# A DiT block with experts: the instruction lists ahead of the main loop in a new order

## The chip, the cores and the metric

One core of a Trainium2 chip. The metric is the device time of one execution in microseconds, the median of several runs. A kernel here is one program written engine by engine: TensorE (PE in the profile), VectorE (DVE), ScalarE (ACT), GpSimd (POOL) and SyncE (SP, which issues the loads and stores) each run a list of instructions in order, and semaphores hold an instruction until what it needs is there.

## The reference

Four sequences of 1024 tokens with 256 channels go through two layers, all in float32:

```python
m = silu(mod) @ w_ada + b_ada              # nine modulation rows per batch
h = ln(x) * (1 + sc_msa) + sh_msa
x = x + self_attn(h) * g_msa               # 16 heads, windows of 128, rolled by 64
h = ln(x) * (1 + sc_mca) + sh_mca
x = x + topk_cross_attn(h, context) * g_mca  # 77 keys, softmax over the 16 largest scores
h = ln(x) * (1 + sc_mlp) + sh_mlp
x = x + swiglu(h) * g_mlp                  # hidden 1024
# second layer
nx = layer_norm(x, gamma, beta)
evidence = softmax(nx @ Wq @ (ctx @ Wk).T / 16) @ (ctx @ Wv)
combined = concat(nx, evidence, cond)
p = softmax(combined @ router_W + router_b)          # three experts
routed = sum_e p_e * (silu(combined @ e_w1[e] + e_b1[e]) @ e_w2[e] + e_b2[e])
g = sigmoid(silu(combined @ gate_w1 + gate_b1) @ gate_w2 + gate_b2)
out = x + g * (routed @ out_w + out_b)
```

## The kernel before, in words

The 4096 tokens are 16 units of 256 tokens (two tiles of 128). A unit passes three stages: A (self-attention), C (cross-attention with the search for the 16 largest of 77 scores) and B (SwiGLU, then the experts). The main loop, `both`, runs stage A of one unit, C of the unit before and B of the one before that side by side. Ahead of the loop `prologue` takes unit 0 through A and C and unit 1 through A, and meanwhile prepares the weights. Only this part is changed.

What is prepared, the "folds": the nine modulations from the condition vector ("mS" for the first norm, "mR" for the others, lines 1014 and 1024); the gate rows of the three residuals ("g25", "g8") and the value biases through the output weights ("bv"); the second expert weights multiplied by the output weight, for which they are first turned ("t00" to "t21", line 688) and then multiplied ("p00" to "p21", line 696); the experts' output biases through the output weight ("b01", "b2", line 645); the turned wk and wq and their product ("wk", "wq", "MT"); the condition's part of the experts' first layer ("anchor", line 674) and of the router ("r0", then "r1", lines 628 and 637).

Three things set the order of the work:

- each engine's list is written out by hand: the calls in `prologue` of TensorE (line 1011), ScalarE (1504), GpSimd (1860) and VectorE (2321). A call that waits holds everything behind it on its engine;
- the eight PSUM banks. Banks 5 to 7 go round among the folds in the order of `FOLD_JOBS` (line 404): a fold may begin when the one three places ahead of it has been read out. `FOLDS_DONE` gives the order in which TensorE ends them. Banks 0 to 4 belong to the stages, in the order of `PRO_JOBS` (line 65): in bank 1 the values of unit u ("v") are followed by slot 1 of its scores ("s01"), so the scores (line 817) wait until ScalarE has copied the values out (line 1394);
- SP's list (line 444). Once VectorE has made the gate rows (line 2034, signal `rows_gated`), SP stores them in device memory and reloads them spread over the partitions, then loads the weights of stage B; once the expert rows are halved (line 2052, `expert_rows`) it stores and reloads these and loads the evidence weights and the down weights.

Self-attention of a unit goes like this: scores into banks 0 to 3 (four slots of four heads), row maxima by VectorE (line 2148), exponentials with row sums by ScalarE (line 1400, sixteen per tile), probabilities turned by TensorE (line 835) and copied out by ScalarE (line 1409), products with the values (line 858). The inverse row sums are spread over the channels by GpSimd (line 1773), turned by TensorE (line 861), copied by ScalarE and multiplied in by VectorE (line 2179); then the projection (line 872). GpSimd's list has, ahead of the first spread, the gating of two output weights with the reloaded gate rows (lines 1862 to 1868). In cross-attention the scores are copied out (line 1424), searched by VectorE in two halves per slot (line 2202: the eight largest, knock them out, the next eight), shifted by GpSimd, put through the exponential by ScalarE (line 1429) and masked by VectorE ("pick", line 2226). `idle_in_values` and `idle_products` (lines 1000 to 1009) are products of the identity whose results nobody reads.

At the end of the prologue, TensorE turns the last probabilities of unit 1 with the router rows between them, and the router rows wait until VectorE has read "r0" (line 640), which stands behind all of unit 0's searches in VectorE's list:

```python
                a_turn_probs(1, 2, 1)
                fold_router_rows()
                a_turn_probs(1, 3, 1)
                wait_folds(pe)
                idle_products(5)
                a_turn_inverses("r1", "pv", 1)
                a_values(1, 1)
```

Of the kernel before, what the change touches and what calls it, by code (L numbers as in the profile page):

```python
# [144 lines left out]
def bass_pixart_experts(nc, x, cond, ctx_in, w_ada, b_ada, w_qkv, b_qkv, w_so, b_so, w_q, b_q, w_kv, b_kv,  # L145
# [6 lines left out]
    with ExitStack() as stack:  # L152
# [182 lines left out]
        def wait_free(eng, name, u):  # L335

            eng.wait_ge(drained[JOB[name][0]], before(name, u) + 1)
# [51 lines left out]
        def every_batch(dst, v):  # L389
# [15 lines left out]
            "cols", "mS", "cT", "cK", "cV", "mR", "bv", "g25", "g8", "t01", "t00", "b01",  # L405
            "anchor", "p00", "p01", "t10", "t11", "b2", "wk", "p11", "p10", "wq", "t20", "t21",
# [3 lines left out]
            "cols", "mS", "cT", "cK", "cV", "mR", "bv", "g25", "g8", "t01", "t00", "b01",  # L410
            "p00", "p01", "anchor", "t10", "t11", "b2", "wk", "p11", "p10", "wq", "t20", "t21",
# [12 lines left out]
        def fold_psum(name):  # L424
            return psum[5 + FOLD_BANK[name]]
# [153 lines left out]
        def _(pe):  # L579
# [116 lines left out]
            def fold_second(e, k2):  # L696

                pe.wait_ge(out_scaled, 1)
                wait_read(pe, f"t{e}0")
                wait_read(pe, f"t{e}1")  # L700
                bk = fold_bank(f"p{e}{k2}")
                for k in (2 * k2, 2 * k2 + 1):
                    for h in range(CB):
                        m = pe.matmul(bk[:, (k % 2) * C:(k % 2 + 1) * C], e2T[h][:, k * P:(k + 1) * P], outw[:, h, :],
                                      start=(h == 0), stop=(h == CB - 1))
                m.then_inc(fold_full, 1)
# [304 lines left out]
            def prologue():  # L1011
# [9 lines left out]
                a_v(0, 0)  # L1021
                context_values(0, fold_bank("cV"))
                a_v(1, 0)
                modulations("mR", (4, 3, 7, 6))
                a_scores(0, range(SLOTS), 0)
                value_biases()
                gate_sections("g25", (0, 1))
                a_turn_probs(0, 0, 0)
                a_turn_probs(0, 1, 0)
                gate_sections("g8", (2,))  # L1030
                a_turn_probs(0, 2, 0)
                fold_turn_second(0, 1)
                a_turn_probs(0, 3, 0)
                fold_turn_second(0, 0)
                fold_expert_biases("b01", (0, 1))
# [4 lines left out]
                idle_in_values(3)  # L1040
                a_turn_probs(1, 1, 0)
                fold_second(0, 0)
                a_turn_probs(1, 2, 0)
                a_turn_probs(1, 3, 0)
                fold_second(0, 1)
# [13 lines left out]
                fold_turn("wk", wk_sb)  # L1059
                pe.wait_ge(readA, 2)  # L1060
                a_cross_scores(0, range(SLOTS), 0)
                wait_free(pe, "pv", 1)
                idle_in_values(2)
                a_turn_input(1)
                idle_in_values(5)
                a_cross_scores(1, range(SLOTS), 0)
# [3 lines left out]
                a_v(0, 1)  # L1070
                fold_second(1, 1)
                a_v(1, 1)
                fold_second(1, 0)
                a_scores(0, range(SLOTS), 1)
# [3 lines left out]
                fold_qk()  # L1078
                a_turn_probs(0, 0, 1)
                fold_router_anchor()  # L1080
                idle_in_values(2)
# [5 lines left out]
                idle_in_values(6)  # L1087
                a_scores(1, range(SLOTS), 1)
                a_values(0, 1)
                fold_second(2, 1)  # L1090
                fold_second(2, 0)
                a_turn_probs(1, 0, 1)
# [264 lines left out]
        def _(act):  # L1357
# [146 lines left out]
            def prologue():  # L1504
# [13 lines left out]
                a_copy_turned(0, 3, 0, "p")  # L1518
                read_fold("t00", e2T[0], fold_psum("t00")[:, :])
                read_fold("t01", e2T[1], fold_psum("t01")[:, :])  # L1520
# [28 lines left out]
                a_kept_exp(0, 0)  # L1549
# [9 lines left out]
                a_copy_turned(0, 3, 1, "p")  # L1559
                a_cross_exp(1, 0, 0)  # L1560
                read_fold("t21", e2T[1], fold_psum("t21")[:, :])
                a_cross_exp(1, 1, 0)
# [4 lines left out]
                a_exp(1, 3, 1)  # L1567
                a_copy_turned(1, 0, 1, "p")
# [1101 lines left out]
```

## Time and profile before

| | |
|---|---|
| device time, median of 3 runs | 1445.8 us (1445.67 to 1449.09) |
| the profiled execution | span 1447.1 us, 30246 instructions; the page gives no other time of it |
| first matmul of the loop (line 920) | 126.78 us after the span's start |
| PE busy | 1413.0 us, 98% |
| DVE busy | 1061.7 us, 73% |
| ACT busy | 837.8 us, 58% |
| POOL busy | 437.8 us, 30% |
| chain that ended last, by engine | PE 83%, DVE 12%, issue 2%, ACT 1% |

"Busy" is time in which an engine executes an instruction. In a timeline, a row is one instruction or several like ones in a row: its start, how long, the engine, the line, the operation with its output and inputs, how many; in brackets how long the engine stood idle before it and who released it. A matmul of float32 shows as two instructions. Starts of consecutive rows may lie closer than the durations, since matmuls overlap at their ends. In a table by stretch each engine has its busy time and its count of instructions, then come the granted share of TensorE's clock (PEclk, 1.00 is 2.4 GHz, 0.50 is 1.2 GHz), the share of the DMA engines and the GB/s.

### The profile page before, as it was taken

How to read it: one execution, taken by the hardware profiler on the slowest of the kernel's cores; microseconds unless marked ns; L12 is line 12 of the kernel's file. 1: busy time of each engine (PE TensorE's matmuls, PEld its weight loads, DVE VectorE, ACT ScalarE, POOL GpSimd, SP SyncE). 2: the span in 40 equal slices, each digit the busy share in tenths (PEclk: the TensorE clock that was granted, in tenths of full speed). 3: DMA queues.
4: the chain of work that ended last, by engine and by line, in shares of the span. 5: the costliest groups of instructions: out<-in, count | busy, mean ns of one | idle time of the engine just before them, and what ended most of it. 6: DMA issues, size and time to landing. Idle time of an engine off the chain costs nothing.

```text
span 1447.1 us, 30246 instructions
## 1 busy us (share of the span) xinstructions
PE 1413.0 (98%) x9777; PEld 1195.1 (83%) x9777; DVE 1061.7 (73%) x4754; ACT 837.8 (58%) x2555; POOL 437.8 (30%) x599
## 2 busy tenths in 40 slices
PE   7999999999999999999999999999999999999997
PEld 5778788888888888888888788888888878887886
DVE  3585869688796878879696777959688786968642
ACT  3464475757566384755757466574757547574433
POOL 1314132333325232332335232233334313232302
PEclk9999999999999999999999999999999999999999
DMA  7520000010000000010010000000010000000000
GB/s 244 196 73 2 1 1 25 1 34 9 19 31 15 1 2 25 2 34 2 21 36 2 15 2 16 11 15 20 8 43 8 16 2 1 9 2 8 1 2 14
DMA packets 27342, 34.99 MB, mean 24 GB/s; under 512 B 3325, under 2 KB 22449, under 8 KB 26930
## 3 DMA queue, kind: packets, MB, share of 16 engines
q1 hardware_dynamic: 27185, 33.07, 7.1%
q8 instruction: 79, 1.29, 0.4%
q14 instruction: 78, 0.63, 0.1%
HBM read 28.83 MB, written 4.22 MB: 23 GB/s over the span
## 4 chain that ended last, share of the span: by engine, by line
PE 83%; DVE 12%; issue 2%; ACT 1%; SPq 0%; POOL 0%; DMA 0%; DVEq 0%; ACTq 0%; POOLq 0%
PE bank L965 13%; PE bank L920 12%; PE bank L989 10%; PE bank L972 7%; PE bank L791 6%; PE bank L929 6%; PE bank L777 4%; PE bank L852 4%; PE bank L840 4%; PE bank L904 4%; DVE knocked L2224 3%; PE bank L830 2%; PE bank L748 2%; PE bank L762 2%; PE bank L812 1%
## 5 line engine op out<-in xcount | busy, mean ns | idle before, releaser
L920 PE MATMUL bank<-hB,Wm 128*128 128x256 f32 x1024 | 242.3, 383 | 2.2 <-ACT hB L1366 2.2
L920 PEld LDWEIGHTS bank<-hB,Wm 128*128 128x128 f32 x1024 | 190.6, 190 | 33.4 <-issue 7.0
L965 PE MATMUL bank<-nxT,W1nx 128*128 128x256 f32 x896 | 212.1, 382 | 0.0
L1405 ACT ACTIVATE prob<-bank,rmax 128x128 f32<-128x128 f32 x512 | 180.3, 432 | 28.3 <-DVE rmax L2151 28.3
L1762 POOL TENSOR_TENSOR scores<-scores,M 128x308 f32<-128x308 f32 x128 | 94.5, 738 | 320.1 <-DVE knocked L2224 317.7
L1412 ACT ACTIVATE probT<-bank 128x512 f32<-128x512 f32 (+1 forms) x256 | 140.3, 617 | 83.8 <-PE bank L904 76.8
L989 PE MATMUL bank<-W2p,gT 128*128 128x256 f32 x768 | 183.2, 381 | 3.0 <-DVE acc L2303 1.9
L965 PEld LDWEIGHTS bank<-nxT,W1nx 128*128 128x128 f32 x896 | 166.1, 191 | 23.1 <-issue 2.8
L989 PEld LDWEIGHTS bank<-W2p,gT 128*128 128x128 f32 x768 | 141.2, 190 | 23.8 <-issue 2.8
L1450 ACT ACTIVATE tbs<-bank,b1half 128x256 f32<-128x256 f32 x128 | 60.7, 474 | 143.1 <-PE bank L920 102.2
L1466 ACT ACTIVATE tbs<-bank,betaH 128x256 f32<-128x256 f32 x224 | 95.6, 489 | 82.7 <-PE bank L972 82.7
L1405 ACT ACTIVATION_READ_ACCUMULATOR prob<-bank,rmax 128x1 f32 x512 | 139.0, 272 | 0.0
L1754 POOL TENSOR_SCALAR vare<-mv 128x2 f32<-128x2 f32 x64 | 17.7, 276 | 385.1 <-DVE mv L2127 382.7
L929 PE MATMUL bank<-Wm_g,gT 128*128 128x256 f32 x480 | 115.2, 380 | 0.0
L972 PE MATMUL bank<-wT,Vp 77*128 77x256 f32 x448 | 114.0, 382 | 0.0
L2224 DVE MATCH_REPLACE8 knocked<-M,scores 128x77 f32<-128x77 f32 x512 | 108.7, 226 | 0.9 <-issue 0.5
L2224 DVE MATCH_REPLACE8 knocked<-M,knocked 128x77 f32<-128x77 f32 x512 | 108.8, 227 | 0.7 <-issue 0.5
L929 PEld LDWEIGHTS bank<-Wm_g,gT 128*128 128x128 f32 x480 | 90.7, 190 | 15.8 <-issue 4.2
L972 PEld LDWEIGHTS bank<-wT,Vp 77*128 77x128 f32 x448 | 81.3, 190 | 14.3 <-issue 4.8
L2151 DVE TENSOR_REDUCE rmax<-bank 128x4 f32<-128x512 f32 x128 | 80.7, 685 | 7.4 <-PE bank L830 7.4
L2217 DVE MAX8 M<-knocked 128x8 f32<-128x77 f32 x512 | 83.8, 227 | 0.3 <-issue 0.3
L2212 DVE MAX8 M<-scores 128x8 f32<-128x77 f32 x512 | 83.7, 227 | 0.1
(238 smaller groups left out, 2772.4 us busy)
## 6 DMA issues: line engine op xcount, KB each, us to landing
Wm_g<-in_L_xcond_w_m_dram SPq DMA_DIRECT2D x4, 1024.0 KB, 5.4
W1ev<-in_L_xcond_e_w_dram SPq DMA_DIRECT2D x6, 512.0 KB, 7.2
x<-in_x_dram SPq DMA_DIRECT2D x16, 128.0 KB, 2.6
x<-in_x_dram SPq DMA_DIRECT2D x32, 64.0 KB, 2.3
Wm<-in_L_xcond_w_m_dram SPq DMA_DIRECT2D x1, 2048.0 KB, 9.3
out_dram<-acc SPq DMA_DIRECT2D x16, 128.0 KB, 1.7
out_dram<-acc SPq DMA_DIRECT2D x32, 64.0 KB, 2.0
batch_rows<-row_store SPq DMA_DIRECT2D x4, 384.0 KB, 3.9
```

The lines of the kernel that those rows point to most:

```text
L791: m = pe.matmul(bk[:, t * C:(t + 1) * C], src[:, k, t * P:(t + 1) * P], w[:, k, :], start=(opens and k == 0 and t == 0), stop=(k == nk - 1 ...
L920: m = pe.matmul(bank_of(name)[:, half * UT:(half + 1) * UT], Wm1[:, k, c:c + P], hB[:, k, :], start=(k == 0), stop=(k == CB - 1))
L929: m = pe.matmul(bank_of("mo")[:, t * C:(t + 1) * C], gated_of(u)[:, j, t * P:(t + 1) * P], Wm2_g[:, j, :], start=(j == 0 and t == 0), stop ...
L965: pe.matmul(bank_of(name)[:, n * UT:(n + 1) * UT], W1nx[:, k, c0 + n * P:c0 + (n + 1) * P], nxT[:, k, :], start=(n == 0 and k == 0), stop= ...
L972: m = pe.matmul(bank_of(name)[:, n * UT:(n + 1) * UT], Vp[:, c0 + n * P:c0 + (n + 1) * P], wT[:, :], start=False, stop=True, skip_group_ch ...
L989: m = pe.matmul(bank_of(name)[:, t * C:(t + 1) * C], hE[:, e % 2, k, t * P:(t + 1) * P], W2p[:, e * RB + k, :], start=(k == 0 and t == 0), ...
L1405: m = act.activation(prob[:, s, i, :], psum[s][:, i * P:(i + 1) * P], ACT.Exp, bias=rmax[:, t, s * HPS + i:s * HPS + i + 1], accum_out=rsu ...
L1412: act.activation(probT[0:np_, s], psum[s][0:np_, :].rearrange("p (i q) -> p i q", i=HPS), ACT.Copy)\
L1466: act.activation(tb[tb_of(name)][:, n * UT:(n + 1) * UT], bank_of(name)[:, n * UT:(n + 1) * UT], ACT.Tanh, bias=betaH[:, n0 + n:n0 + n + 1 ...
L1762: pool.tensor_tensor(Dx[:, t, g, :], S[:, t, g, :], M12[:, t, g, 0:1].to_broadcast([P, HPS, LC]), ALU.subtract)\
L2217: dve.max(M12[:, t, h, 8:TOPK], K[:, h, :]).then_inc(topk, 1)
L2224: dve.match_replace(K[:, h, :], top, src, KNOCKED).then_inc(topk, 1)
```

## The change

Only the order of calls changes, and one fold can be done in halves. On TensorE: unit 0's first scores move ahead of the context's values and the modulations "mR"; the four turned slots of probabilities are spread among the folds that follow; "p00" and "p01" are done in two halves each, one behind each turned slot, and three idle products go; the biases of experts 0 and 1 ("b01") move behind unit 0's first cross scores, and the turn of wk behind unit 1's values; of the 26 idle products in the bank of the weighed values 11 are left. On VectorE: unit 0's first row maxima move ahead of the context's values and the modulations; "b01", the halving of the expert rows and the copy of "wk" come among the searches; unit 1's row maxima come earlier among the searches. On ScalarE some exponentials and copies change place. GpSimd's and SP's lists stay, though SP now waits for signals that come at other points of the other lists. The diff, cut to its core:

```diff
 FOLD_JOBS = [
-    "cols", "mS", "cT", "cK", "cV", "mR", "bv", "g25", "g8", "t01", "t00", "b01",
-    "anchor", "p00", "p01", "t10", "t11", "b2", "wk", "p11", "p10", "wq", "t20", "t21",
+    "cols", "mS", "cT", "cK", "cV", "mR", "bv", "g25", "g8", "t01", "t00",
+    "anchor", "p00", "p01", "t10", "t11", "b2", "b01", "wk", "p11", "p10", "wq", "t20", "t21",
     "MT", "r0", "p21", "p20", "r1",
...
 FOLDS_DONE = [
-    "cols", "mS", "cT", "cK", "cV", "mR", "bv", "g25", "g8", "t01", "t00", "b01",
-    "p00", "p01", "anchor", "t10", "t11", "b2", "wk", "p11", "p10", "wq", "t20", "t21",
+    "cols", "mS", "cT", "cK", "cV", "mR", "bv", "g25", "g8", "t01", "t00",
+    "p00", "p01", "anchor", "t10", "t11", "b2", "b01", "wk", "p11", "p10", "wq", "t20", "t21",
     "MT", "r0", "p21", "p20", "r1",
...
-    def fold_second(e, k2):
-        pe.wait_ge(out_scaled, 1)
-        wait_read(pe, f"t{e}0")
-        wait_read(pe, f"t{e}1")
-        bk = fold_bank(f"p{e}{k2}")
-        for k in (2 * k2, 2 * k2 + 1):
+    def fold_second(e, k2, halves=(0, 1)):
+        if 0 in halves:
+            pe.wait_ge(out_scaled, 1)
+            wait_read(pe, f"t{e}0")
+            wait_read(pe, f"t{e}1")
+            fold_bank(f"p{e}{k2}")
+        bk = fold_psum(f"p{e}{k2}")
+        for half in halves:
+            k = 2 * k2 + half
             for h in range(CB):
-                m = pe.matmul(bk[:, (k % 2) * C:(k % 2 + 1) * C], e2T[h][:, k * P:(k + 1) * P], outw[:, h, :],
+                m = pe.matmul(bk[:, half * C:(half + 1) * C], e2T[h][:, k * P:(k + 1) * P], outw[:, h, :],
                               start=(h == 0), stop=(h == CB - 1))
-        m.then_inc(fold_full, 1)
+        if 1 in halves:
+            m.then_inc(fold_full, 1)
...
         a_v(0, 0)
+        a_v(1, 0)
+        a_scores(0, range(SLOTS), 0)
         context_values(0, fold_bank("cV"))
-        a_v(1, 0)
         modulations("mR", (4, 3, 7, 6))
-        a_scores(0, range(SLOTS), 0)
+        a_turn_probs(0, 0, 0)
         value_biases()
+        a_turn_probs(0, 1, 0)
         gate_sections("g25", (0, 1))
-        a_turn_probs(0, 0, 0)
-        a_turn_probs(0, 1, 0)
+        a_turn_probs(0, 2, 0)
         gate_sections("g8", (2,))
-        a_turn_probs(0, 2, 0)
+        a_turn_probs(0, 3, 0)
         fold_turn_second(0, 1)
-        a_turn_probs(0, 3, 0)
         fold_turn_second(0, 0)
-        fold_expert_biases("b01", (0, 1))
         a_scores(1, range(SLOTS), 0)
...
         a_turn_probs(1, 0, 0)
-        idle_in_values(3)
+        fold_second(0, 0, (0,))
         a_turn_probs(1, 1, 0)
-        fold_second(0, 0)
+        fold_second(0, 0, (1,))
         a_turn_probs(1, 2, 0)
+        fold_second(0, 1, (0,))
         a_turn_probs(1, 3, 0)
-        fold_second(0, 1)
+        fold_second(0, 1, (1,))
         a_values(1, 0)
...
         fold_expert_biases("b2", (2,))
-        fold_turn("wk", wk_sb)
         pe.wait_ge(readA, 2)
         a_cross_scores(0, range(SLOTS), 0)
+        a_turn_input(1)
+        fold_expert_biases("b01", (0, 1))
+        a_cross_scores(1, range(SLOTS), 0)
         wait_free(pe, "pv", 1)
-        idle_in_values(2)
-        a_turn_input(1)
-        idle_in_values(5)
-        a_cross_scores(1, range(SLOTS), 0)
         idle_in_values(2)
...
         a_v(0, 1)
+        a_v(1, 1)
+        fold_turn("wk", wk_sb)
         fold_second(1, 1)
-        a_v(1, 1)
+        a_scores(0, range(SLOTS), 1)
         fold_second(1, 0)
-        a_scores(0, range(SLOTS), 1)
         fold_turn("wq", wq_sb)
...
         fold_turn_second(2, 1)
-        fold_qk()
         a_turn_probs(0, 0, 1)
-        fold_router_anchor()
-        idle_in_values(2)
+        idle_in_values(3)
         a_turn_probs(0, 1, 1)
...
         a_turn_probs(0, 3, 1)
-        idle_in_values(6)
+        fold_qk()
+        fold_router_anchor()
         a_scores(1, range(SLOTS), 1)
...
         fold_second(2, 1)
+        a_turn_probs(1, 0, 1)
         fold_second(2, 0)
-        a_turn_probs(1, 0, 1)
         a_turn_probs(1, 1, 1)
...
         a_copy_turned(0, 3, 0, "p")
+        read_fold("t01", e2T[1], fold_psum("t01")[:, :])
         read_fold("t00", e2T[0], fold_psum("t00")[:, :])
-        read_fold("t01", e2T[1], fold_psum("t01")[:, :])
         a_exp(1, 0, 0)
...
         read_fold("p10", W2p[:, 1 * RB + 0:1 * RB + 2, :].rearrange("p k c -> p (k c)"), fold_psum("p10")[:, :])
-        a_kept_exp(0, 0)
         read_fold("wq", wqT[:, :, :].rearrange("p h c -> p (h c)"), fold_psum("wq")[:, :])
...
         a_copy_turned(0, 3, 1, "p")
+        a_kept_exp(0, 0)
+        read_fold("t21", e2T[1], fold_psum("t21")[:, :])
         a_cross_exp(1, 0, 0)
-        read_fold("t21", e2T[1], fold_psum("t21")[:, :])
-        a_cross_exp(1, 1, 0)
         read_fold("MT", MT[:, :, :].rearrange("p h c -> p (h c)"), fold_psum("MT")[:, :])
...
         a_exp(1, 3, 1)
+        a_cross_exp(1, 1, 0)
         a_copy_turned(1, 0, 1, "p")
...
         a_bias_queries(0)
+        a_max(0, (0,), 0)
+        a_max(0, (1,), 0)
+        a_max(0, (2,), 0)
+        a_max(0, (3,), 0)
         context_values(0, fold_psum("cV"))
...
         prep_m(0)
-        a_max(0, (0,), 0)
-        a_max(0, (1,), 0)
-        a_max(0, (2,), 0)
-        a_max(0, (3,), 0)
         dve.wait_ge(folded_loaded, 16 * len(folded_loads))
...
         gate_bias_rows()
-        dve.wait_ge(fold_full, FOLD_FULL["b01"])
-        expert_bias("b01", (0, 1))
         a_max(1, (0,), 0)
...
         expert_bias("b2", (2,))
-        read_fold("wk", wkT[:, :, :].rearrange("p h c -> p (h c)"), fold_psum("wk")[:, :])
-        halve_expert_biases()
         a_topk("a", 0, 0, 0)
         a_topk("a", 0, 1, 0)
+        dve.wait_ge(fold_full, FOLD_FULL["b01"])
+        expert_bias("b01", (0, 1))
         a_topk("b", 0, 0, 0)
+        halve_expert_biases()
         a_topk("a", 0, 2, 0)
...
         a_topk("b", 0, 1, 0)
+        read_fold("wk", wkT[:, :, :].rearrange("p h c -> p (h c)"), fold_psum("wk")[:, :])
         a_topk("b", 0, 2, 0)
...
         a_topk("a", 1, 0, 0)
-        a_topk("b", 0, 3, 0)
-        a_topk("a", 1, 1, 0)
         a_max(0, (0,), 1)
...
         a_max(0, (3,), 1)
+        a_topk("b", 0, 3, 0)
+        a_topk("a", 1, 1, 0)
         a_topk("b", 1, 0, 0)
...
         a_topk("b", 1, 1, 0)
+        a_max(1, (0,), 1)
+        a_max(1, (1,), 1)
+        a_max(1, (2,), 1)
+        a_max(1, (3,), 1)
         a_topk("a", 1, 3, 0)
...
         a_topk("b", 1, 3, 0)
-        a_max(1, (0,), 1)
-        a_max(1, (1,), 1)
-        a_max(1, (2,), 1)
-        a_max(1, (3,), 1)
         a_pick(1, 1, 0)
...
         read_fold("p21", W2p[:, 2 * RB + 2:2 * RB + 4, :].rearrange("p k c -> p (k c)"), fold_psum("p21")[:, :])
```

## Rows read from the trace of the kernel before

**Rows 1.** Busy time, granted clock (PEclk) and DMA by stretch of the whole run

```profile
28.50:33.50 5.00, 5.00 (x22) 1.60 (x19) 3.98 (x10) 3.83 (x23) 0.00 (x0) 0.66 0.68 247
...
59.00:64.00 5.00, 4.65 (x19) 3.77 (x18) 2.28 (x6) 1.02 (x2) 4.42 (x8) 0.66 0.49 120
...
99.50:108.50 9.00, 8.32 (x66) 7.54 (x67) 2.21 (x8) 4.99 (x18) 1.48 (x4) 0.62 0.36 117
...
126.70:1447.00 1320.30, 1302.43 (x8920) 1104.92 (x8918) 993.78 (x4444) 777.29 (x2352) 407.77 (x538) 1.00 0.04 12
```

**Rows 2.** PE timeline, 23-40 us: start, duration, engine, line, operation, tiles, count

```profile
23.36 1.03 PE L812 MATMUL bank<-Wqkv,hA 128*128 128x256 f32 x4
...
24.23 0.28 PE L605 MATMUL bank<-siluT,W1nx 128*128 128x4 f32 x2
...
27.79 1.15 PE L830 MATMUL bank<-km,qT 32*128 32x256 f32 x16
...
37.97 1.89 PE L652 MATMUL bank<-Wm_g,cols 128*1 128x256 f32 x8
...
39.79 1.15 PE L830 MATMUL bank<-km,qT 32*128 32x256 f32 x16
```

**Rows 3.** Timeline of VectorE: last instruction of the gate rows

```profile
38.15 0.28 DVE L2040 TENSOR_SCALAR nxT<-nxT 4x256 f32<-4x256 f32 x1
```

**Rows 4.** Timeline of GpSimd: the inverses spread for the first unit

```profile
49.48 0.74 POOL L1783 COPY xnA<-rinv 128x256 f32<-128x256 f32 x2
```

**Rows 5.** Timeline of PE: inverses turned, first cross scores

```profile
50.76 0.66 PE L869 MATMUL bank<-ident,xnA 128*128 128x128 f32 x4
...
65.64 0.81 PE L894 MATMUL bank<-kc,qT 32*128 32x154 f32 x16
```

**Rows 6.** Timeline of PE, 67 to 80 us, second unit

```profile
67.44 1.28 PE L1009 MATMUL bank<-ident 128*128 128x128 f32 x10
...
76.33 1.03 PE L812 MATMUL bank<-Wqkv,hA 128*128 128x256 f32 x4
...
79.02 1.15 PE L830 MATMUL bank<-km,qT 32*128 32x256 f32 x16
```

**Rows 7.** Timeline of ScalarE, 77 to 103 us

```profile
77.64 0.59 ACT L1396 ACTIVATE va<-bank 128x512 f32<-128x512 f32 x1
...
83.38 0.37 ACT L1405 ACTIVATE prob<-bank,rmax 128x128 f32<-128x128 f32 x1 [0.61 <-DVE rmax L2151]
...
95.83 0.37 ACT L1405 ACTIVATE prob<-bank,rmax 128x128 f32<-128x128 f32 x1 [2.10 <-DVE rmax L2151]
...
101.33 1.66 ACT L1412 ACTIVATE probT<-bank 128x512 f32<-128x512 f32 x3
```

**Rows 8.** Timeline of VectorE: folds, last search, last maxima, router row

```profile
39.90 0.86 DVE L2047 SCALAR_TENSOR_TENSOR Vp<-bank,out_row 1x256 f32<-1x256 f32 x2 [1.47 <-PE bank L652]
...
65.75 0.69 DVE L1993 COPY Wm_g<-bank 128x512 f32<-128x512 f32 x1 [0.18 <-PE bank L661]
...
66.36 0.54 DVE L2056 TENSOR_SCALAR Vp<-Vp 1x768 f32<-1x768 f32 x1
...
93.72 0.65 DVE L2217 MAX8 M<-knocked 128x8 f32<-128x77 f32 x4
...
95.11 2.48 DVE L2151 TENSOR_REDUCE rmax<-bank 128x4 f32<-128x512 f32 x4
...
97.50 0.79 DVE L2231 SCALAR_TENSOR_TENSOR scores<-knocked,scores 128x616 f32<-128x616 f32 x1
...
99.73 0.14 DVE L2418 TENSOR_TENSOR rrow<-bank,rrow 4x3 f32<-4x3 f32 x1
```

**Rows 9.** Timeline of the DMA queue of SP: loads behind the expert rows

```profile
68.51 1.46 SPq L528 DMA_DIRECT2D W1ev<-in_L_xcond_e_w_dram  x3
```

**Rows 10.** Timeline of PE: router rows, first picked scores turned

```profile
100.77 1.86 PE L642 MATMUL bank<-rrow,onehot 4*128 4x3 f32 x8
...
108.04 1.97 PE L904 MATMUL bank<-ident,scores 128*77 128x128 f32 x16
```

## The prediction

> **What bounds the kernel now.** I read the page first, then busy time and granted clock by stretch, then the timelines of the four engines over the first 127 us, where all of the change lies. From 126.70 us on TensorE is busy for 1302.43 of 1320.30 us at full clock [rows 1]: the loop is TensorE's and hardly waits. So whatever moves the loop's first matmul (start 126.7 us) moves the end of the run by as much, and nothing else that the change does counts. In front of the loop there are three things to see. First, TensorE is nearly always occupied, yet its clock stands at half in three stretches: a share of 0.66 over 5 us means 2 x 0.34 x 5 = 3.4 us at 1.2 GHz, twice, and 0.62 over 9 us means 6.8 us [rows 1]; all the rest runs at 2.4 GHz. Second, from 67 to 100 us VectorE works without a pause (the searches), and ScalarE waits 2.10 us for it before the second unit's last exponentials [rows 7]. Third, TensorE meets the end of that list at the router rows, 100.77 us, for which VectorE's row at 99.73 was ready 0.9 us before [rows 8, 10].
>
> **The change, part by part.**
>
> *First scores ahead of the modulations.* Now the scores start at 27.79, behind a value product and the modulations, 24.23 to 27.79 = 3.56 us [rows 2]. The second value product moves ahead of the context's, 0.87 us earlier (24.23 - 23.36 [rows 2]), so it ends at 23.4. But slot 1 of the scores lies in the bank of the values, and ScalarE must copy them out first, 0.59 us [rows 7]; before, the modulations hid that. The scores start at about 24.2 and TensorE waits some 0.75 us. VectorE's maxima and the exponentials start 3.5 us earlier. Behind them TensorE does the same work in another order, less the expert-bias fold of 39.79 - 37.97 = 1.82 us [rows 2], plus the wait: the second scores come 1.82 - 0.75 = 1.1 us earlier (bounds: 0.5 if the wait is 1.3, 1.8 if there is none).
>
> *What that does to the gate rows.* The third gate product now stands behind three groups of turned probabilities instead of two, and behind the wait: 0.75 + 0.5 (four transposes start to start; 0.66 with their tail [rows 5]) = 1.25 us later. VectorE finishes the rows at 38.15 + 0.28 = 38.43 [rows 3]; SP stores and reloads them, GpSimd gates two weights and then spreads the inverses until 49.48 + 0.74 = 50.22 [rows 4]. That chain of 11.8 us is of fixed steps, so the spread ends at 51.5. TensorE turned the inverses at 50.76 [rows 5], its own work being last by 0.54 us; now it is there at 50.76 - 1.1 = 49.7 and waits 1.8 us. The earlier exponentials are lost here: the projection and the normalisation behind it come 0.7 us later (bounds: 0.5 earlier if the gate rows are not late, 1.3 later if the cover of 0.54 is already gone).
>
> *The halved second folds and the three idle products that go.* The four halves are the same matmuls, placed between probabilities that wait for ScalarE: nothing, while those exponentials last 101.33 - 95.83 = 5.5 us [rows 7]; without that cover each half costs 0.87.
>
> *Two folds behind the cross scores.* The turn of wk leaves the way of the first cross scores, -0.5 us: 65.64 becomes 65.64 + 0.7 - 0.5 = 65.85 [rows 5]. The bias fold, 1.82 us, replaces idle products worth 1.37 (67.44, ten instructions [rows 6]): +0.45. For SP the expert rows come some 5 us later and with them the store, the reload and the evidence weights, now issued from 68.51 [rows 9], and the down weights behind them; all are wanted only at the loop, 50 us on, so nothing.
>
> *The second unit.* The fold whose end is 76.33 [rows 6] now stands behind the second value product (0.87) and the wk turn (0.5): it ends at 76.33 + 0.2 + 0.45 + 0.87 + 0.5 = 78.35. ScalarE's list is not changed there: it reads that fold, does a cross exponential and only then copies the values, which ended 1.9 us behind the fold (77.64 + 0.59 - 76.33 [rows 6, 7]). So the scores, which need the bank, start at 80.3 instead of 79.02 [rows 6]. Behind them TensorE does a second fold (1.74), two turns (1.0) and ScalarE reads all three before the exponentials: 80.3 + 1.1 + 1.74 + 1.0 + 0.6 = 84.7, against 83.38 [rows 7]. The row maxima moved among the searches are ready at about 82, and ScalarE makes nothing of it. Exponentials 5.5, copies 2.1: the second tile's scores start at 92.3, their maxima at 93.5, against 95.11 [rows 8].
>
> *VectorE's list.* It gains what stood in free time before: two bias rows 0.86, the halving 0.54, the wk copy 0.6 [rows 8], together 2.0 us. It loses none. Ahead of the last maxima now stand three searches and a pick fewer; a search is 95.11 - 93.72 = 1.39, a pick 0.7 [rows 8], so 4.9 us are put behind them. Its work ahead would be done at 95.11 + 0.2 + 2.0 - 4.9 = 92.4, and it waits until 93.5. From there 99.87 - 95.11 = 4.76 of old work and 4.9 of moved work follow [rows 8]: the router row is ready at 103.2. With no stall it would be 102.1, with all delays above doubled 105.
>
> *The end of it.* TensorE's router rows wait for that row and stand ahead of the last turned probabilities: 103.3 instead of 100.77, though those exponentials are over earlier. From the router rows to the turned picks it took 108.04 - 100.77 = 7.27 us [rows 10], all at half clock [rows 1]. Bounds: 7.27 again, or 4.2 at full clock (the steps of VectorE and GpSimd between do not shrink). Two of three half-clock stretches were 3.4 us long, which would lie in this part and give 7.27 - 1.7 = 5.6; I take that. The picks are turned at 108.9, 0.9 us later, and what follows to the loop is not touched.
>
> **Sum:** +0.9, taken as +1 us. The profiled execution has a span of 1447.1 us and is 1.3 above the median of 1445.8; a difference of the two kernels is applied to the median: 1446.8 us. A measurement of this kernel tells about 0.3%, 4.3 us, from no change.
>
> **Rivals.**
> *Slower: a fourth half-clock stretch.* Place: TensorE's new wait of 1.8 us ahead of the turned inverses, followed by anchor products of four columns and the projection. Modulations of the same four columns stood right ahead of the first half-clock stretch [rows 1, 2], which speaks for it; against it, that block was 3.56 us in one piece [rows 2], and here four transposes and the wait lie between the products. Price: the anchors and the projection at half for 3.4 to 6.8 us, 1.7 to 3.4 lost, and with the router rows later still the last part at 7.27, another 1.6: +1 + 2.5 + 1.6 = +5, 1450.9 us. [...] The Trainium skill ("TensorE: Matmul & The Clock Gate", section "HAM oscillation — how this bites in real kernels") holds that waits between bursts let the clock fall and the next burst starts cold; by that rule this case is the likelier one. The rows agree only in part: the first stretch had no wait ahead of it.
> *Faster: fewer half-clock stretches.* If the scores ahead of the modulations spare the first stretch (1.7 us, and the gate rows come that much earlier) and the router rows run at full clock (1.4), +1 becomes -2 to -4: 1442.8 us. For it: the scores and the context's values now stand right ahead of the modulations. Against: the same four-column block of 3.56 us remains in one piece.
> *The moved maxima pay.* If the router row did not hold TensorE, the last exponentials, 1.5 us earlier, would set the end: 1444.3 us. Against: VectorE's list is only longer.
>
> **How the numbers follow.** Forecast 0.6, slower rival 0.2, faster rival 0.12, moved maxima 0.08. Over 0.3% faster is the outer half of the faster rival, 0.07; over 0.3% slower nearly all of the slower one and a tail of the forecast's doubled delays, 0.2; the rest, 0.73, is within. The range leaves out a tenth at each side: from 1442.8 (the faster rival) to 1451.0 (the slower).
>
> **What would show it.** Right: the first scores near 24.2 with a wait on the values' copy; a wait of 1 to 2 us on GpSimd's spread before the turned inverses; the second unit's scores at 80 behind the values' copy; VectorE pausing before its last maxima; TensorE waiting over 2 us for the router row near 103; the loop starting near 127.7. Wrong: the inverses turned before 50.5, the router row before 101, or a different number of half-clock stretches.

## The result, and the profile after

The changed kernel takes 1459.6 us (median of 4 runs, 1457.39 to 1460.03) against 1447.37 for the kernel before in the same session (4 runs); the ratio is 1.0069 [1.0051, 1.0087] (the medians alone give 12.2 us or 0.85%, inside that interval). By the bound of 0.3% it is slower, and the time lies above the predicted range. The profiled execution took 1460.03 us, its span is 1458.2 us: 11.1 more than before. The loop is what it was, and only starts later: its first matmul at 137.72 instead of 126.78 us. So 10.9 us have to be found ahead of it.

First the busy time and the granted clock by stretch (as in [rows 1]: the stretch, its length, busy time of PE, PEld, DVE, ACT and POOL, granted clock, DMA share, GB/s); the last row but one lies between the inverses that TensorE turns for the first unit and the first cross scores, the last one is the loop:

```profile
28.50:33.50 5.00, 5.00 (x26) 3.49 (x26) 2.34 (x13) 4.21 (x23) 0.93 (x2) 0.61 0.69 247
33.50:59.00 25.50, 23.31 (x184) 16.88 (x183) 8.05 (x15) 11.00 (x42) 4.83 (x8) 0.83 0.45 157
59.00:64.00 5.00, 5.00 (x20) 4.46 (x19) 1.69 (x5) 0.00 (x0) 0.29 (x2) 0.50 1.07 369
99.50:108.50 9.00, 8.40 (x86) 6.66 (x84) 6.56 (x35) 8.39 (x39) 0.70 (x1) 1.00 0.01 2
53.59:73.24 19.65, 19.50 (x81) 17.12 (x81) 5.33 (x16) 2.45 (x5) 6.03 (x12) 0.57 0.67 229
137.70:1458.00 1320.30, 1303.05 (x8919) 1105.56 (x8918) 993.69 (x4444) 775.82 (x2351) 407.13 (x538) 1.00 0.04 12
```

In the loop TensorE's busy time is 1303.05 us in an equally long stretch, against 1302.43 [rows 1]. From 59 to 64 us the clock is 0.50, the lower level throughout. The row from 53.59 on says 0.57: 2 x 0.43 x 19.65 = 16.9 us at 1.2 GHz (17.1 by finer cuts, from 53 to 71). The kernel before has three stretches at that level ahead of the loop, of 3.4, 3.4 and 6.8 us [rows 1]; this one has 6.8 (29 to 36), 17.1 and 6.8 (111 to 118). In all 30.7 us against 13.6, so 17.1 more, worth half of that, 8.5 us, where TensorE works without a pause.

The same part before, cut at the same two matmuls ([rows 5] has their starts):

```profile
50.76:65.64 14.88, 13.83 (x88) 11.67 (x84) 5.92 (x16) 2.46 (x5) 6.80 (x13) 0.89 0.75 249
```

TensorE is busy 13.83 us there at a clock of 0.89; after, 19.50 at 0.57, for a little less work (the turn of wk left this part). Now TensorE's marks in the changed kernel (timeline: start, duration, engine, line, operation, tiles, count, idle time before and what ended it):

```profile
24.68 1.15 PE L834 MATMUL bank<-km,qT 32*128 32x256 f32 x16 [0.99 <-ACT va L1398]
...
41.16 1.15 PE L834 MATMUL bank<-km,qT 32*128 32x256 f32 x16
...
50.83 1.08 PE L856 MATMUL bank<-probT,va 128*32 128x128 f32 x32 [0.52 <-ACT probT L1414]
53.59 1.11 PE L873 MATMUL bank<-ident,xnA 128*128 128x128 f32 x4 [1.68 <-POOL xnA L1785]
54.49 3.41 PE L683 MATMUL bank<-condT,W1ev 128*128 128x4 f32 x16
57.76 3.76 PE L795 MATMUL bank<-Wso_g,hA 128*128 128x256 f32 x8
...
73.24 0.81 PE L898 MATMUL bank<-kc,qT 32*128 32x154 f32 x16
...
87.98 1.15 PE L834 MATMUL bank<-km,qT 32*128 32x256 f32 x16 [2.08 <-ACT va L1398]
...
111.95 1.84 PE L642 MATMUL bank<-rrow,onehot 4*128 4x3 f32 x8 [4.05 <-DVE rrow L2420]
...
119.00 1.21 PE L908 MATMUL bank<-ident,scores 128*77 128x128 f32 x9
...
137.72 1.99 PE L924 MATMUL bank<-hB,Wm 128*128 128x256 f32 x8
```

These answer to [rows 2, 5, 6, 10]. Four waits of about 1 us and more are new: 0.99 and 2.08 us for ScalarE's copy of the values, 1.68 for GpSimd's spread, 4.05 for VectorE's router row. Besides, a wait of 0.52 us stands one group of products ahead of the one for the spread, and the one for unit 1's first exponentials is 1.65 us instead of 0.55. Behind the wait for the spread, the turned inverses take 1.11 us instead of 0.66 [rows 5], and the anchor products run at half: the 44 that stand behind the inverses, grouped, first before, then after (columns: line, operation, tiles, count, then busy time and mean duration).

```profile
L683 PE MATMUL bank<-condT,W1ev 128*128 128x4 f32 x44 | 5.0, 249 | 0.0
```

```profile
L683 PE MATMUL bank<-condT,W1ev 128*128 128x4 f32 x44 | 9.4, 348 | 0.0
```

The 44 anchors cost 4.4 us more, and the projection takes 3.76 us for its eight instructions, against 1.97 at full clock in the run with the wait taken away, below. VectorE's and GpSimd's marks, which answer to [rows 3, 4, 8]:

```profile
41.75 0.28 DVE L2042 TENSOR_SCALAR nxT<-nxT 4x256 f32<-4x256 f32 x1
...
101.94 2.48 DVE L2153 TENSOR_REDUCE rmax<-bank 128x4 f32<-128x512 f32 x4 [2.56 <-PE bank L834]
...
111.66 0.14 DVE L2420 TENSOR_TENSOR rrow<-bank,rrow 4x3 f32<-4x3 f32 x1
```

```profile
52.78 0.74 POOL L1785 COPY xnA<-rinv 128x256 f32<-128x256 f32 x2
```

Cutting the time ahead of the loop at TensorE's marks shows where the 10.9 us are:

| part, from start to start | before, us | after, us | difference | forecast |
|---|---|---|---|---|
| start to turned inverses | 50.76 | 53.59 | +2.83 | +0.7 |
| to the first cross scores | 14.88 | 19.65 | +4.77 | -0.5 |
| to the second unit's scores | 13.38 | 14.74 | +1.36 | +1.1 |
| to the router rows | 21.75 | 23.97 | +2.22 | +1.25 |
| to the turned picks | 7.27 | 7.05 | -0.22 | -1.65 |
| to the loop | 18.74 | 18.72 | 0 | 0 |

### The profile page after: what moved, and what is told of

Its sections match the earlier page's. It is cut to its first block, busy times and chain, and to the rows that moved or that the text cites. A ratio compares the mean times of both kernels' runs of the same rounds, so it can differ in the third digit from the quotient of the medians.

```text
span 1458.2 us, 30186 instructions
## 1 busy us (share of the span) xinstructions
PE 1417.6 (97%) x9747; PEld 1198.7 (82%) x9747; DVE 1061.2 (73%) x4754; ACT 836.1 (57%) x2555; POOL 437.1 (30%) x599
## 4 chain that ended last, share of the span: by engine, by line
PE 83%; DVE 11%; issue 2%; ACT 2%; DMA 0%; POOL 0%; SPq 0%; DVEq 0%; POOLq 0%; ACTq 0%
PE bank L969 12%; PE bank L924 12%; PE bank L993 10%; PE bank L976 7%; PE bank L795 6%; PE bank L933 6%; PE bank L781 4%; PE bank L856 4%; PE bank L908 3%; PE bank L844 3%; DVE knocked L2226 3%; PE bank L834 2%; PE bank L766 2%; PE bank L752 2%; PE bank L816 1%
```

## The experiments

The theory after the two profiles: the wait ahead of the turned inverses drops TensorE's clock, and what follows it then runs at half for 17 us. The rival: a wait costs its own length, and the long stretch comes from something else in the new order. I give each experiment's part from the turned inverses to the first cross scores, because no later part disturbs it.

**The wait taken away.** The changed kernel with GpSimd's spread ahead of the gating of the output weights, which does not need it.

```diff
                 rstd_of(0, EPS0, 1)
+                a_spread("pv", 0)
                 wait_read(pool, "bv")
...
                 gate_co(0)
-                a_spread("pv", 0)
                 rstd_of(1, EPS0, 0)
```

> The changed kernel with GpSimd spreading the first unit's inverses ahead of gating the weights instead of behind it. Theory (the wait of 1.7 us for the spread, with the four-column anchor products behind it, sets off the 17 us at half clock from 53.5 us): the inverses are turned right behind the weighed values, near 52.0 instead of 53.6; the long half-clock stretch is gone or as short as the 3.4 us of before; first cross scores near 66.5 instead of 73.2; loop near 131 instead of 137.7; about 1453 us. Rival (the anchors and the missing idle products bring the clock down whether or not there is a wait): the stretch stays, only the wait is saved, 1458 us.

1452.6 us (10 runs, 1451.07 to 1454.43), ratio 1.0030 [1.0019, 1.0041]: 7.0 us below the changed kernel by the medians, 0.39% or 5.6 by the ratios. Timeline of TensorE and the part behind the inverses:

```profile
51.11 0.66 PE L873 MATMUL bank<-ident,xnA 128*128 128x128 f32 x4
51.60 1.85 PE L683 MATMUL bank<-condT,W1ev 128*128 128x4 f32 x16
53.34 1.97 PE L795 MATMUL bank<-Wso_g,hA 128*128 128x256 f32 x8
```

```profile
51.11:64.83 13.72, 12.90 (x84) 11.10 (x81) 5.52 (x16) 2.45 (x5) 7.84 (x14) 0.88 0.96 334
```

No wait for the spread, no long stretch, anchors and projection at full speed; the loop starts at 129.25 us in this profile, 8.5 earlier than in the changed kernel's. More than half of the loss hangs on this wait.

**The wait filled.** The changed kernel with seven idle products (fourteen instructions in the row) ahead of the turned inverses, so that TensorE does not pause; the inverses come no earlier.

```diff
                 a_values(1, 0)
+                idle_in_bank(3, 7)
                 a_turn_inverses("r1", "pv", 0)
```

> The changed kernel with seven idle products of the identity (some 1.9 us) between the weighed values and the turned inverses, in a bank that is free there: the wait keeps its length, TensorE is busy in it. Theory: inverses still turned near 53.6, but no half clock behind; projection near 55.9 instead of 57.8, first cross scores near 68, loop near 133, about 1455 us. Rival (the wait's length, not TensorE's idleness, is what costs, or the anchors bring the clock down): same as the changed kernel, 1459 us.

1456.64 us (4 runs, 1454.19 to 1457.07), 1.0055 [1.0035, 1.0075].

```profile
52.11 1.83 PE L1018 MATMUL bank<-ident 128*128 128x128 f32 x14
53.78 0.60 PE L873 MATMUL bank<-ident,xnA 128*128 128x128 f32 x4
```

```profile
53.78:68.74 14.96, 14.57 (x83) 12.38 (x81) 5.52 (x16) 2.46 (x5) 6.62 (x13) 0.77 0.77 265
```

The inverses are as late as in the changed kernel (53.78), yet the part behind them takes 14.96 us: the lateness alone does not cost those 5 us, the pause does. The clock of 0.77 is a stretch of 6.8 us at half from 60 us on. The reading rests on this part and not on the times alone, for the interval of the ratio overlaps the changed kernel's. By the medians the time falls by only 3.0 us: the part is 4.7 us shorter, but from the second unit's scores to the router rows it takes 25.6 us instead of 23.97, with a new stretch of 3.4 us at half at 84 us, behind the wait for the values.

**The wait made in the kernel before**, where nothing is reordered: GpSimd copies the inverses six times more, into a tile not yet in use, ahead of its spread.

```diff
                 gate_co(0)
+                pool.wait_ge(sums_inverted, 1)
+                for i in range(6):
+                    pool.tensor_copy(scores[:, i * C:(i + 1) * C]..., rinv[:, 0, :]...)
                 a_spread("pv", 0)
```

> The kernel before with six more copies on GpSimd (0.37 us each, into a tile not in use) ahead of the first spread, 2.2 us: nothing else changes. TensorE gets a wait of about 1.7 us ahead of the turned inverses. Theory: that wait alone starts a long half-clock stretch near 53 us; the loop starts 5 to 8 us later, 1453 to 1455 us. Rival: 1.7 us later and no more, 1449 us.

1449.76 us (10 runs), 1.0011 [0.9997, 1.0025]. The wait came out at only 1.08 us, and no long stretch follows in the profile:

```profile
54.75 0.66 PE L869 MATMUL bank<-ident,xnA 128*128 128x128 f32 x4 [1.08 <-POOL xnA L1783]
```

```profile
54.75:69.03 14.28, 13.58 (x85) 11.59 (x85) 5.84 (x16) 2.45 (x5) 5.94 (x12) 0.88 0.77 256
```

Here the rival's number was right, and the theory's missed. Seven of the ten runs took 1449.4 to 1449.8 us. The profile is of one of the other three (1452.1 us, granted clock over the whole run 0.992). The last two, 1454.2 and 1455.3 us, have 0.990 and 0.988, which with two levels means some 6 and 12 us more at half than in the profiled one. Where these lie is not known, so a wait of this length may start a long stretch in some executions. The test was repeated with nine copies:

> The kernel before with nine more copies on GpSimd ahead of the first spread (3.3 us; six gave TensorE a wait of 1.1 us, no long stretch in the profile and 1449.8 us). Theory (a wait of about 2 us starts the long half-clock stretch, one of 1 us mostly not): wait of 2 to 3 us, a stretch of 10 us or more at half clock from about 53 us, 1455 to 1458 us. Rival (the long stretch needs something else of the changed kernel): only the wait more, 1451 us.

1456.63 us (6 runs, 1455.01 to 1457.73), 1.0055 [1.0038, 1.0071].

```profile
52.36 0.66 PE L869 MATMUL bank<-ident,xnA 128*128 128x128 f32 x4 [2.59 <-POOL xnA L1783]
52.85 2.61 PE L683 MATMUL bank<-condT,W1ev 128*128 128x4 f32 x16
55.33 3.76 PE L791 MATMUL bank<-Wso_g,hA 128*128 128x256 f32 x8
```

```profile
52.36:72.53 20.17, 20.14 (x85) 17.12 (x85) 5.65 (x16) 2.46 (x5) 7.37 (x14) 0.58 0.39 124
...
1365.00:1405.00 40.00, 36.84 (x164) 31.57 (x164) 15.27 (x33) 13.10 (x33) 10.02 (x10) 0.96 0.00 1
```

This decides between the two. A wait of 2.59 us, alone, in the old order, and the part behind it takes 20.17 us at a clock of 0.58, 5.3 more than before; the changed kernel's 19.65, with the turn of wk (0.5) gone from it, is 5.3 more too. The loop starts 5.3 us later than before (the inverses themselves are 1.6 later, and the part from the router rows to the picks is 1.55 shorter). The other 3 us of this profile lie at the far end of the run, where two more stretches of 3.4 us at half stand, one of them in the last row (0.96, where the kernel before has 1.00). They are not the edit's alone: the run with the router row read early, below, has no such copies and two stretches of 3.4 us at 1380 and 1422 us as well (a clock of 0.72 over 6 us each).

**The change cut in two.** The front alone (all edits up to `a_values(1, 0)`, with the bias fold left in its old place), and the rest alone.

Against the kernel before, in TensorE's list, the front first:

```diff
                 a_v(0, 0)
+                a_v(1, 0)
+                a_scores(0, range(SLOTS), 0)
                 context_values(0, fold_bank("cV"))
-                a_v(1, 0)
                 modulations("mR", (4, 3, 7, 6))
-                a_scores(0, range(SLOTS), 0)
...
```

```diff
-                fold_expert_biases("b01", (0, 1))
                 a_scores(1, range(SLOTS), 0)
...
                 a_cross_scores(0, range(SLOTS), 0)
...
                 a_turn_input(1)
+                fold_expert_biases("b01", (0, 1))
...
```

> Of the change only the front: first scores ahead of the modulations with their maxima, the turned slots among the folds, the halved second folds. Bias fold, wk turn, searches and maxima of the second unit stay as before. Theory: the front makes the larger part of the loss: gate rows near 41.5 instead of 38.4, wait before the turned inverses, half clock behind; first cross scores 6 to 8 us later than before, 1454 to 1455 us. Rival (the part behind the cross scores makes the loss): within 2 us of before, 1449 us.

> Of the change only the part from the bias fold on: bias fold and wk turn behind the first cross scores, the second unit's order, maxima among the searches. The front is that of before, so the gate rows are on time, but TensorE, without the bias fold of 1.8 us, may reach the turned inverses that much earlier. Theory (the long half-clock stretch needs late gate rows and an early TensorE together; the back by itself costs the longer list of VectorE): a wait of at most 1.3 us before the turned inverses, no long stretch; the router rows wait about 4 us for VectorE's row; loop 2 to 4 us later than before, 1450 to 1453 us. Rival (the missing bias fold alone opens the wait and with it the long stretch): 1456 us or more.

The front alone took 1453.22 us (10 runs), 1.0030 [1.0016, 1.0044]; the rest alone 1451.02 (10 runs, 1449.44 to 1458.49), 1.0029 [1.0009, 1.0049]. Neither profile shows a wait for the spread. With the bias fold in place TensorE is at the inverses at 54.49, behind GpSimd's spread (the row below: over at 54.20), so the wait that the theory had for the front alone is not there; the 3.7 us by which TensorE is later than before are most of the loss (4.2 by the medians of that session). Without the new front the spread is on time and the inverses come at 48.98. In these profiles the long stretch needs both halves: late gate rows from the one, an earlier TensorE from the other. For every execution this is not shown: two of the ten runs of the rest alone took 1458.5 us at a granted clock of 0.988, against 0.993 in the profiled one (1450.91 us). That is some 15 us more at half, about what the long stretch would add, and a time that the rival had named; where they lie is not known. The rest alone shows the second unit's parts of the changed kernel without its front: 14.74 us from the cross scores to the second unit's scores, and a wait of 4.04 for the router row.

```profile
53.46 0.74 POOL L1788 COPY xnA<-rinv 128x256 f32<-128x256 f32 x2
```

**What is left: two repairs in the second unit**, each on top of the early spread. First ScalarE's copy of the values ahead of the cross exponential and the fold's read:

```diff
+                a_copy_values(1)
                 a_cross_exp(0, 0, 0)
                 read_fold("p11", ...)
                 a_cross_exp(0, 1, 0)
-                a_copy_values(1)
```

> The changed kernel with the spread ahead of the gating (1452.6 us) and ScalarE copying the second unit's values before it reads the fold p11 and does the first cross exponentials. Theory (the values' copy behind p11 holds the second unit's scores by 2.1 us and with them VectorE's last maxima): scores near 77.5 instead of 79.6, VectorE's pause before its last maxima 1 us or less instead of 2.6, router row 1 to 2 us earlier, 1451 us. Rival (the scores are held by something else, or VectorE's list swallows it): 1452.6 us.

Then instead the router row read right behind the last maxima, and the inverse sums right behind the last pick:

```diff
                 a_max(1, (3,), 1)
+                dve.wait_ge(folded_loaded, 16 * len(folded_loads))
+                dve.wait_ge(fold_full, FOLD_FULL["r0"])
+                read_done("r0", ...)
                 a_topk("a", 1, 3, 0)
...
                 a_pick(1, 1, 0)
+                a_invert_sums(1)
```

> The changed kernel with the spread ahead of the gating (1452.6 us) and VectorE reading the router row right behind its last maxima instead of behind the picks and two folds, and inverting the second unit's sums right behind the last pick. Theory (TensorE's wait of 4.0 us for that row, with half clock behind it, is the rest of the loss): no wait at the router rows, last probabilities turned near 101, half-clock stretch there shorter or gone, loop 2 to 5 us earlier, 1448 to 1450 us. Rival (VectorE's list ends too late anyway, the wait only moves to the turned inverses): 1452 us.

The first: 1450.03 us (10 runs), 1.0011 [1.0000, 1.0022], 2.6 below the early spread alone by the medians. From the cross scores to the second unit's scores it took 12.59 us instead of 14.78, and the router row still came 24.0 behind those scores, with the wait of 4.04:

```profile
79.25 1.15 PE L834 MATMUL bank<-km,qT 32*128 32x256 f32 x16
...
103.23 1.84 PE L642 MATMUL bank<-rrow,onehot 4*128 4x3 f32 x8 [4.04 <-DVE rrow L2420]
```

The loop of this profile starts at 129.10, only 0.15 earlier than with the early spread alone, since a stretch at half between the inverses and the cross scores was 6.8 us long instead of 3.4 and that part 1.6 us longer.

The second: 1453.74 (10 runs), 1.0029 [1.0015, 1.0043]. Nothing gained: the router rows no longer wait, but TensorE then waits one group of turned probabilities later, for VectorE's read of the router biases, which stands behind the reads of two folds:

```profile
102.59 1.05 PE L642 MATMUL bank<-rrow,onehot 4*128 4x3 f32 x8
...
107.00 1.35 PE L1007 MATMUL bank<-ident 128*128 128x128 f32 x10 [2.76 <-DVE rbias_all L2423]
```

So both repairs together, and that last read brought forward, with TensorE waiting for it alone:

```diff
                 a_turn_probs(1, 3, 1)
-                wait_folds(pe)
+                wait_read(pe, "r1")
...
                 a_pick(1, 1, 0)
+                dve.wait_ge(fold_full, FOLD_FULL["r1"])
+                read_done("r1", ...)
+                a_invert_sums(1)
```

> The changed kernel with all repairs: spread ahead of the gating, values copied first, router row read behind the last maxima, router biases and inverse sums right behind the last pick, and TensorE waiting before its idle products for the read of the router biases alone (with the router row alone the wait had only moved there, 2.8 us). Theory (these three waits and the half clock behind them are the whole loss): at or below the kernel before, 1446 to 1448 us. Rival (the first scores ahead of the modulations and the longer list of VectorE cost by themselves): 1450 us.

1446.08 us (12 runs, 1444.55 to 1446.95), 0.9980 [0.9970, 0.9990]: the whole loss is undone.

```profile
98.48 1.05 PE L642 MATMUL bank<-rrow,onehot 4*128 4x3 f32 x8
...
101.06 1.65 PE L1007 MATMUL bank<-ident 128*128 128x128 f32 x10 [0.94 <-DVE rbias_all L2419]
...
105.36 2.00 PE L908 MATMUL bank<-ident,scores 128*77 128x128 f32 x16
```

By parts: turned inverses 50.65, then 15.37, 12.59, 19.87, 6.88 and 18.75 us, 13.6 less than the changed kernel in all; the medians differ by 13.5.

**The useful piece alone.** The kernel before with the last maxima ahead of the last searches and VectorE's reads ordered as above (with TensorE's wait for the last read alone, and one of ScalarE's cross exponentials moved as in the change), without and with the early spread.

```diff
                 a_topk("b", 1, 1, 0)
+                a_max(1, (0,), 1)
...
+                read_done("r0", ...)
                 a_topk("a", 1, 3, 0)
                 a_topk("b", 1, 2, 0)
                 a_pick(1, 0, 0)
                 a_topk("b", 1, 3, 0)
-                a_max(1, (0,), 1)
...
                 a_pick(1, 1, 0)
+                read_done("r1", ...)
+                a_invert_sums(1)
```

> The kernel before with one thing of the change, the second unit's last maxima ahead of the last searches, and what lets it pay: router row read behind them, router biases and inverse sums behind the last pick, TensorE waiting before its idle products for the router biases alone. Theory: last exponentials 2 to 3 us earlier, no wait at the router rows, the half clock of 6.8 us at 100 us shorter: loop 3 to 5 us earlier, about 1444 us. Rival (TensorE's waits only move and the half clock stays): 1447 to 1448 us.

> As the run with the last maxima ahead in the kernel before, with the first unit's spread ahead of the gating too. Theory (in the kernel before the spread is ready 0.5 us ahead of TensorE, so nothing waits): same time as without, within 1 us, but a narrower spread of the runs. Rival: another 1 to 2 us earlier.

1445.97 us, 0.9984 [0.9971, 0.9998], and 1445.85, 0.9981 [0.9969, 0.9994] (12 runs each). TensorE's marks in the first of the two:

```profile
81.89 1.15 PE L830 MATMUL bank<-km,qT 32*128 32x256 f32 x16
...
101.10 1.05 PE L642 MATMUL bank<-rrow,onehot 4*128 4x3 f32 x8
...
106.41 1.97 PE L904 MATMUL bank<-ident,scores 128*77 128x128 f32 x16
```

From the second unit's scores to the picks it is 19.2 + 5.3 = 24.5 us in both, against 29.0 before. Part of these 4.5 us is the clock, as neither profile has a stretch at half at the router rows; by the medians of the session (1448.96 for the kernel before) it is 3.0 us. They end where the repaired change ends: a gain of some 0.2%, with intervals that leave out 1 but less than the 0.3% of my bound. So what can pay in this change are the moved maxima with the reads behind them in order (the maxima alone were not run on the kernel before); the early spread adds nothing that these runs can tell.

## Why the prediction was wrong, step by step

**The step that failed is the price of the new wait at the turned inverses.** The sum took that wait at its length (+0.7 us at the inverses, then -0.5 to the first cross scores) and put half clock behind it at nothing. Half clock was left to the slower rival, with a chance of 0.2 and "the anchors and the projection at half for 3.4 to 6.8 us, 1.7 to 3.4 lost", sized by the lengths of the stretches in the trace of before. The runs showed 17.1 us at half, and the part behind the wait grew by 5.3 us. The rival's place, cause and sign were right: a wait of 1.8 us (1.68 measured) and half clock in anchors and projection. Against it I had held that "four transposes and the wait lie between the products"; the wait was no relief, it was the cause. None of it followed a wait of 1.08 us in the profiled execution, and all of it 1.68 and 2.59. One of the signs that I named was blind to it: the number of half-clock stretches ahead of the loop is three as before, only they last 30.7 us instead of 13.6.

The Trainium skill ("TensorE: Matmul & The Clock Gate", section "HAM oscillation — how this bites in real kernels") describes a kernel in which TensorE waits for loads after each burst, for some 3 to 5 us, its clock falls, and the next burst starts cold. The runs show the same behind shorter waits: the part takes 13.72 us with the wait taken away, 19.65 behind 1.68 us and 20.17 behind 2.59. In the prediction I did not say that the waits of that kernel are longer. And I set the rule back behind the first stretch of before, which no wait precedes; that stretch shows that there are other causes, not that a wait is none.

**The gate rows and the first part: half right.** They ended at 42.03 instead of 38.43, 3.6 us later where I took 1.25, and the second scores started at 41.16 instead of the forecast 38.7. Both sides of the wait slipped alike, so the wait itself came out as forecast. Of the 2.4 us missed, 0.5 is the later start of the first scores (24.68 for 24.2; the wait for the values' copy was 0.99 for 0.75), and most of the rest the first stretch at half, 6.8 us long instead of 3.4: 1.7. In the run with the early spread that stretch was 3.4, and from first to second scores it took 14.92 us, against 38.7 - 24.2 = 14.5 by my sum and 16.48 in the changed kernel's profile. I had carried the first stretch over as a constant; it is not one (last section).

**Right:** the second unit's scores held by the values' copy behind the fold's read (+1.36 for +1.1; taking it away gave 2.2 us); VectorE pausing ahead of its last maxima (2.56 us); the router row late for TensorE (a wait of 4.05, "over 2 us").

**Sizes off in the second unit:** to the router rows +2.22 for +1.25. From there to the picks I expected 5.6 us, with half the clock loss of before; it was 7.05, as that stretch again was 6.8 long. The bound of 7.27 held it; the other bound, 4.2 at full clock, was too low: with no stretch there that part took 5.3 us (the moved maxima on the kernel before).

**Rivals.** "The moved maxima pay" did not come true in the change, for the reason given (VectorE's list is only longer), but is what the last experiments turn into a gain. The faster rival failed: the first stretch was not spared.

The terms, measured minus forecast: 2.1 at the front, 5.3 in the long stretch, 0.3 and 1.0 in the second unit, 1.4 at the picks, together 10.1, which with the forecast 0.9 make the 10.9 found, but for rounding.

**A reading that was off without changing the sum.** I set the span of 1447.1 us against the median device time of 1445.8. The changed kernel's profiled execution took 1460.03 us for a span of 1458.2, so device times are some 1.8 us longer than spans, and the profile of before is of an execution of about 1449 us, one of the two longer of its four runs.

## What to carry to other kernels

Before work is moved, measure the cover of each side chain that TensorE meets: here gate rows, store, reload, gating and spread had 0.54 us in hand, and the change ate it from both ends. Do not price a new TensorE wait at its length alone: here waits of 1.68 and 2.59 us put the work behind them at half clock and cost another 5.3 us each. If such a wait can't be avoided by the order, let an instruction that doesn't need the late data go first on the late engine, which here cost one moved line. A repair that takes away one wait may only show the next (2.76 us, one group of products later): repair the chain to its end before judging it.

## What was not expected of the hardware

TensorE's clock does not fall at the same places in each execution of one list. In the profiles of the kernels that keep the old front, the first stretch at half lasted 3.4 us [rows 1], 6.8 (the six copies; the moved maxima) or was missing (the nine copies; the rest alone; the moved maxima with the early spread), though TensorE's list ahead of it is the same. Each 3.4 us costs 1.7 where TensorE sets the pace, which is of the size by which runs of one kernel differ: the kernel before ran between 1445.9 and 1451.9 us in 25 runs of one session. There the clock tells the runs apart: the nine up to 1447.2 us have a granted clock of 0.995 or 0.996 over the whole run, the sixteen from 1448.8 us on 0.991 or 0.992. A sum with terms below 2 us, as mine, is finer than a single profile of this kernel can bear.

A long stretch went on without any further wait: in the changed kernel TensorE idles 0.15 us (19.65 - 19.50) between the turned inverses and the cross scores and is at half speed for 17 us of it, though it ran the same anchors and projection at full speed in the kernel before.

What stays open: what a wait between 1.08 and 1.68 us does (no run was made; the 1.68 us, unlike the other two waits, also have one of 0.52 us shortly ahead of them), whether the anchors of four columns behind it are needed to keep the clock down, since no run had the wait without them, what the two runs of 1458.5 us of the rest alone had, and what starts the late stretches near 1380 and 1422 us. Each of the stretches was seen in one profile of its kernel.
